# Edge loop of a four-layer graph network: GpSimd, not ScalarE, copies each group's gather indices

## What is computed

```python
def _L0_gnn_ref(h, e, src, dst, W1, b1, W2, b2):
    x = jnp.concatenate([h[src], h[dst], e], axis=1)
    m = jax.nn.relu(x @ W1 + b1) @ W2 + b2
    h_new = jax.ops.segment_sum(m, dst, num_segments=h.shape[0])
    return h_new
...
# layer 1
    msg = jax.nn.relu(x[src] + edge_attr @ We + be)
    aggr = jax.ops.segment_sum(msg, dst, num_segments=x.shape[0])
    h = (1.0 + eps_gin) * x + aggr
    h = jax.nn.relu(h @ W1 + b1) @ W2 + b2
...
# layers 2 and 3: 3 and 10 steps of this kind, with normalised edge weights
    agg = jax.ops.segment_sum(h[s] * wn[:, None], d, num_segments=n)
```

## Time and profile before

| | |
|---|---|
| median of 3 runs | 2695.18 us (2695.15 to 2700.47) |
| profiled execution, its time | 2692.2 us |
| its span | 2690.4 us |
| mean granted clock of TensorE | 0.984 |
| TensorE busy | 2607.0 us, 97% |
| DVE busy | 1788.8 us, 66% |
| GpSimd busy | 1169.4 us, 43%, of it 1146.5 in 1,212 gathers |
| ScalarE busy | 420.2 us, 16%, 1,080 instructions |
| DMA | 447.32 MB, 166 GB/s over the span |

### The profile page before, as it was taken

One profiled execution on the slowest core, in us unless ns is written; L12 is line 12 of the kernel. 1 busy time (PEld: TensorE's weight loads), 2 busy tenths in 40 slices (PEclk: granted clock), 3 DMA queues, 4 the chain that ended last, 5 costly groups with the idle time before them and its releaser, 6 DMA issues.

```text
span 2690.4 us, 59886 instructions
## 1 busy us (share of the span) xinstructions
PE 2607.0 (97%) x18663; PEld 1739.0 (65%) x18663; DVE 1788.8 (66%) x3713; ACT 420.2 (16%) x1080; POOL 1169.4 (43%) x1235
## 2 busy tenths in 40 slices
PE   6899999999999799999999999899999999999998
PEld 5688888888888578888888888533333333333333
DVE  4688888888888599999999999796531111111114
ACT  2122222222222211111111111200100000000001
POOL 4466666666666367777777777200000000000000
PEclk9899999999999799999999999799999999999999
DMA  4222222222222333333333333299999999999997
GB/s 110 52 62 60 60 60 60 61 60 60 59 61 60 61 69 86 77 77 77 78 78 79 78 93 80 83 348 365 341 336 346 351 350 350 351 346 353 359 345 268
DMA packets 376595, 447.32 MB, mean 166 GB/s; under 512 B 154575, under 2 KB 193589, under 8 KB 373290
## 3 DMA queue, kind: packets, MB, share of 16 engines
q1 hardware_dynamic: 323834, 376.76, 43.0%
q0 software_dynamic: 38784, 39.79, 8.0%
q10 hardware_dynamic: 13920, 30.00, 3.0%
HBM read 416.03 MB, written 30.36 MB: 166 GB/s over the span
## 4 chain that ended last, share of the span: by engine, by line
PE 94%; DVE 2%; DMA 1%; ACT 1%; SPq 1%; issue 0%; DVEq 0%; ACTq 0%
PE bank L1577 31%; PE bank L1778 31%; PE bank L1600 11%; PE bank L1589 7%; PE bank L1564 4%; PE bank L1568 3%; PE bank L1749 2%; PE bank L1553 2%; PE bank L1782 1%; DMA arena<-in_edge_weight 1%; SPq L572 0%; PE bank L1736 0%; PE bank L1720 0%; ACT arena L1493 0%; PE bank L1714 0%
## 5 line engine op out<-in xcount | busy, mean ns | idle before, releaser
L1778 PE MATMUL bank<-arena 128*64 128x512 f32 (+1 forms) x4368 | 889.0, 543 | 12.7 <-DVE arena L1087 10.6
L1577 PE MATMUL bank<-arena 128*128 128x320 bf16 x6090 | 882.2, 301 | 8.7 <-DVE arena L840 8.7
L1577 PEld LDWEIGHTS bank<-arena 128*128 128x128 bf16 x6090 | 599.1, 98 | 250.1 <-DVE arena L840 8.9
L658 POOL DMA_INDIRECT arena<-d_p,arena x606 | 573.7, 947 | 299.4 <-issue 240.2
L658 POOL DMA_INDIRECT arena<-d_t,arena x606 | 572.8, 945 | 212.5 <-issue 207.2
L1778 PEld LDWEIGHTS bank<-arena 128*64 128x64 f32 x4368 | 316.2, 136 | 496.7 <-issue 464.3
L1185 DVE TENSOR_TENSOR arena<-bank,arena 128x256 f32<-128x256 f32 (+1 forms) x70 | 27.8, 396 | 572.6 <-PE bank L1749 572.5
L1600 PE MATMUL bank<-arena 128*128 128x150 f32 x2352 | 333.0, 290 | 0.0
L1600 PEld LDWEIGHTS bank<-arena 128*128 128x128 f32 x2352 | 317.8, 189 | 5.3
L847 DVE SCALAR_TENSOR_TENSOR bank<-arena,bank 128x320 f32<-128x320 f32 x404 | 222.7, 552 | 142.5 <-PE bank L1577 142.5
L840 DVE TENSOR_TENSOR arena<-arena,bank 128x1280 bf16<-128x1280 f32 x203 | 299.4, 1475 | 0.0
(11 more groups left out here) (209 smaller groups left out, 1592.9 us busy)
## 6 DMA issues: line engine op xcount, KB each, us to landing
arena<-d_w SPq DMA_DIRECT2D x312, 1024.0 KB, 8.8
arena<-d_code SPq DMA_DIRECT2D x203, 128.0 KB, 3.0
d_w<-arena ACTq DMA_DIRECT2D x24, 1024.0 KB
arena<-in_edge_attr SPq DMA_DIRECT2D x101, 128.0 KB
arena<-d_p,arena POOLq DMA_INDIRECT x606
arena<-d_t,arena POOLq DMA_INDIRECT x606
arena<-d_rec SPq DMA_DIRECT2D x588, 4.0 KB
arena<-d_q SPq DMA_DIRECT2D x202, 11.8 KB
```

What stands on the lines that cost most here:

```text
L658: g.indirect_dma_start(G[:, b, j, 0:F], None, table, bass.IndirectOffsetOnAxis(ap=idx[:, b, j:j + 1], axis=0)).then_inc(r.g[b], 16)
L1577: last = t.matmul(psY[g], SOH[:, g, a_, :], X[:, a_, z, :, :], start=a_ == z == 0, stop=a_ == SLICES - 1 and z == PARTS - 1)
L1778: last = t.matmul(banks[t_ % 4][F * (n % 2):F * (n % 2) + F, 0:w_], old[:, n, :], right, start=n < 2, stop=False)
```

## The change

GpSimd's `superblock` gets two new lines ahead of its waits: from superblock 2 of each stage on it waits until the gathers that last used the buffer have landed, and then it copies the eight index columns itself. The copy raises `r.idx[b]`, the same semaphore as before, and the wait for it stays where it was. ScalarE's copies go, in the loop, before it and at its end. GpSimd waits once for the load of `idxall`.

```diff
+            pool.wait_ge(s.ld_idx, 16)
+
             def superblock(r, i, h, b, k, kh, q, mb, qh, more):
                 table = d_p if r is R[0] else d_t1
+                if not isinstance(i, int) or i >= 2:
+                    pool.wait_ge(r.g[b], 16 * TILES[b][0] * h)
+                g.tensor_copy(idx[:, b, :], idxall[:, ds(8 * i, 8)]).then_inc(r.idx[b], 1)
                 pool.wait_ge(r.idx[b], h + 1)
                 pool.wait_ge(r.seg[b], h + 1)
                 pool.nop(nofuse=True)
...
-            def indices(r, i, b):
-
-                a.activation(idx[:, b, :], idxall[:, ds(8 * i, 8)], ACT.Copy).then_inc(r.idx[b], 1)
-
             def superblock(r, i, h, b, k, kh, q, mb, qh, more):
                 act.wait_ge(r.add[b], h + 1 + 1)
                 rows_ = G[:, b, :, 0:F]
                 a.activation(rows_, rows_, ACT.Relu).then_inc(r.relu[b], 1)
-                if exists(r, i + 2):
-                    indices(r, i + 2, b)
...
-                if layer == 0:
-                    act.wait_ge(s.ld_idx, 16)
-                    for b in range(2):
-                        indices(R[0], b, b)
                 if layer == 0:
                     product_copy(R[layer], 0, 0)
                 edge_loop(act, layer, superblock, quarter_end, None if layer else after)
-                if layer == 0:
-                    for b in range(2):
-                        act.wait_ge(R[0].g[b], 16 * TILES[b][0] * (NSB // 2 + 1 - b))
-                        indices(R[1], b, b)
```

## The result

| | before | after |
|---|---|---|
| median | 2695.16 us (2692.57 to 2700.47, 4 runs) | 2764.26 us (2763.86 to 2765.57, 4 runs) |
| profiled span | 2690.4 us | 2762.8 us |
| TensorE busy | 97% | 95% |
| ScalarE busy | 420.2 us | 400.9 us |
| GpSimd busy | 1169.4 us | 1214.0 us |

The ratio is 1.0256, 95% interval 1.0244 to 1.0269: 69 us slower. The forecast was 2773, 78 us slower, range 2725 to 2835.

A forecast was written before the change was run, and what follows sets the result against it. TensorE bounds the second edge stage at 7.55 us per superblock, GpSimd nearly equal at 7.50. With the longer pause, 71 us (second stage) plus 7 (first) make 78 on the 2695.18 us median: 2773, range 2725 to 2835.

The forecast's parts named there:

- pause of a group: GpSimd's time from a group's last gather to the next group's first: 0.15 + 0.19 + 0.74 = 1.08 us, between 0.83 and 1.32.
- GpSimd has 0.05 us of room in the second stage and 1.00 in the first: Second stage: GpSimd needs 7.50 us per group, TensorE gives 7.55; first stage: a 1.00 us pause, 8.19 - 7.19.
- From a gather's end to the copy: Pause's first term on GpSimd, last gather's end to the copy's start: between 0 and 0.30 us, middle 0.15 taken.
- From its count to the gather: Pause's last term on GpSimd, the copy's count to the next group's first gather: 0.74 us, as after the segment matmul.
- Who is late now: Behind late gathers: DVE's add, ScalarE's relu, then TensorE's segment matmuls; 1.0 us of delay forgiven, once.
- The wait for the landed gathers is free, and ScalarE's relief worth nothing: GpSimd's wait is for a group ended 7 us before; ScalarE loses 202 copies, 38 us, without gain.
- Contention: DVE's two-port work can hold up GpSimd; nothing added at the copy; meeting DVE's own copy every time would add 33 us.
- The rest is unchanged: The part after 1700 us, behind the second edge stage, has no gathers and changes by nothing.
- the clock as a rival inside the stages: TensorE's idle time in the edge stages might drop its clock to 1.2 GHz: up to 1518 us more; chance 0.02.
- The overlapped start: Rival: GpSimd prepares the gather while awaiting the copy, so only 0.19 joins the 0.30 us pause: 2708 us; chance 0.08.
- The cold gather: Rival: each group's first gather behind the copy takes 1.22 us in place of 0.95: 2825 us; chance 0.06.
- The hidden copy: Rival: the copy runs between the previous group's gathers, its count ready before the segment matmul's: price 0, 2695 us; chance 0.05.

The follow-up runs named there:

- e6: The change with one more copy of eight columns ahead of the index copy, both inside the waited chain: 2785.74 us, ratio 1.0332.
- e7: The change, but the next superblock's indices are copied between a group's fourth and fifth gather: 2703.06 us, ratio 1.0027 to the kernel before.
- e5: The kernel before, ScalarE's copies kept, plus an awaited one-column GpSimd memset that nobody reads ahead of each group: 2754.61 us, ratio 1.0217.
- e1: GpSimd copies the indices in the first edge stage alone, ScalarE in the second: 3141.69 us, ratio 0.9985 to the kernel before on a slower chip.
- f1: Same kernel as e1, repeated on another slower chip: 3141.09 us, ratio 0.9983 to the kernel before there.

## Why the prediction was right, point by point

| term | forecast | measured |
|---|---|---|
| pause of a group | 1.08 us | 0.98, in the mean of the second stage 1.01 |
| the six gathers of a group | 7.19 us | 7.21 |
| second stage | +71 | +65.8 |
| first stage | +7 | 0 |
| behind the second stage | 0 | +6.9, not shown to be the change's |
| sum against the profiled execution | +78 | +72.4 |

- *GpSimd has 0.05 us of room in the second stage and 1.00 in the first.* Right, and it decided the result: the same pause of 0.98 us is free in one and costs 66 us in the other. The 1.00 was 0.98 in truth, since a group's gathers now take 7.21 us; the forecast's 1.08 would have made the first stage pay, as e6 shows with 1.10.
- *From a gather's end to the copy: 0.15, between 0 and 0.30.* This was the mis-sized step: it is 0.00 (1301.80 + 0.95 = 1302.75). The 0.30 us between two gathers lie ahead of the second, not behind the first; e7 shows the copy within it.
- *The copy: 0.19.* 0.20.
- *From its count to the gather: 0.74.* 0.78 by the row, since 0.74 was counted from matmuls' modelled ends. In a quarter of the second stage's groups it was 0.89, as at 1312.04, always at the first group of an iteration of the loop. In e5 nearly every first group shows it, with 0.85 to 0.88, in e6 none. That makes 0.03 us in the mean, 3 of the 66 us; its cause stays open.
- *Who is late now.* Only in part right. The path was given as add, relu, segment matmuls; it accounts for 12 us of TensorE's idle time in the second stage. 37 us came by DVE's one-hots for the one-hot gather, which the forecast did not have. For the sum this makes no difference, since GpSimd sets the period by either path.
- *The wait for the landed gathers is free, and ScalarE's relief worth nothing.* The queue's rows for that wait last 0.06 us each and lie one group ahead of the copy (1306.27 for the copy at 1310.94). ScalarE's busy time fell by 19 us and not by 38, since its copies ran half under the relu (1309.28, while the relu of 0.64 us from 1308.74 still ran). e5 keeps ScalarE's copies, has no such wait, and loses 59 us with a shorter operation. What is left for the two is 10 us at most, and the shorter operation accounts for 98 x 0.09 = 9 of them.
- *Contention.* Not seen at the copy, whose length stays 0.20. But DVE's own copy L839 took 0.30 us at 1305.64, beside a gather, in place of 0.17. DVE's lateness had moved it there. In the second stage 17 of these 97 copies took more than 0.20 us, up to 0.41, where none did before. What that adds was not measured apart.
- *The rest is unchanged.* In the profiled executions wrong by 6.9 us, which stood in for the first stage's 7 us that did not come. Two terms failed, and their errors cancel: luck. In the medians it is some 3.6 us, and as this part differs by 5 us between two profiles of one kernel, taken on two chips (e1, f1), it is not shown to come of the change. I had given the clock as a rival inside the stages, where it stayed full as in the earlier trace rows; it was lost behind them instead.
- *The rivals.* The overlapped start falls by the 0.78 in every pause. The cold gather falls too: 0.96 us behind a copy, 0.02 more than before, and not 1.22. The hidden copy falls in the second stage. On the chips where TensorE is held up the copy is hidden indeed, not because it came early, as I had it, but because the matmuls came late.

## What to carry to other kernels

An engine at 43% busy can be a hair from setting the pace of one stage; the pause ahead of its work, beside the pause it needs at least, tells how near. A small operation moved to an engine costs its place in the chain of waits, not its length: put as the last thing ahead of work that awaits it, 0.20 us became 0.62, and two gathers earlier 0.08. So when the producer and the consumer are on one engine, produce for the next round in the middle of this one, and keep the wait for something long done.

## What was unexpected of the hardware

- GpSimd starts a small copy at once behind an indirect DMA, within 0.01 us, and an indirect DMA behind an unawaited copy after 0.16 us. The 0.30 us between two indirect DMAs is room in which a 0.20 us copy costs 0.05, and 0.03 more by the DMA behind it, which takes 0.97 us in place of 0.94.
- Two copies of 0.20 and 0.18 us in a row start 0.13 us apart. In the pause the second one counts with 0.12 us, and not with its duration.
- On two chips the same program takes 3146 us where it took 2695 in the other runs, with TensorE at its full clock in most slices but stopping within groups of matmuls. The second stage's half of the change, which holds all of the 66 us, was within 0.2% of nothing there, so that a verdict holds for the chip that it was measured on.
- After the second stage TensorE's clock was at 1.2 GHz for 34 us in the profile before, 51 in that of the change and of e7, and 48 with the tail filled. One and the same kernel had 37 us in e1 and 48 in f1. What sets this length stays open.
